# Residuals read in place, the context's low half split in two operations, and a second norm worked out from the first one's variance

## The reference, cut to what matters

```
x = x + xattn(ctx, layernorm(x), mask)      # 16 heads of 16, 256 context rows
x = x + attn(layernorm(x))                  # norms once more inside, 16 heads of 64
x = x + ffn(layernorm(x))                   # 256 -> 1024 -> 256, 8 experts
# layernorm(x) = (x - mean) / sqrt(var + 1e-5)
# inside attn: xn = (x - mu) * rsqrt(var(x) + 1e-5) * g + b;  q = xn @ Wq;  k, v = x @ Wkv
```

## Time and profile before

| | us |
|---|---|
| median of 3 runs | 1583.59 |
| lowest and highest run | 1582.69, 1585.09 |
| the profiled execution's own time | 1582.87 |
| its span in the trace | 1581.1 |

### The profile page before, as it was taken

The page is one execution under the profiler, slowest core; times in us unless marked ns, Lnnn a source line. Parts: engine busy times, 40 slices in busy tenths (PEclk is TensorE's granted clock), DMA queues, the critical chain, the costliest instruction groups (busy, mean ns, idle before and its releaser), DMA issues.

```text
span 1581.1 us, 42702 instructions
## 1 busy us (share of the span) xinstructions
PE 1406.5 (89%) x16891; PEld 1024.8 (65%) x16891; DVE 1243.2 (79%) x3414; ACT 1123.3 (71%) x3091; POOL 491.3 (31%) x589
## 2 busy tenths in 40 slices
PE   3378999999999999999999999999999999999975
PEld 1245776766677666666776766667666666776744
DVE  2647888888888888888888888888888888888862
ACT  2656778777777787777778777777787777778741
POOL 2122233333323332333233333323332333233220
PEclk7589999999999999999999999999999999999987
DMA  8522212222221122222212222221122222212100
GB/s 199 171 68 75 64 42 63 70 78 79 79 79 47 43 69 78 79 78 79 70 39 60 69 78 79 78 79 53 42 65 78 78 78 79 75 37 57 52 4 7
DMA packets 80918, 110.49 MB, mean 70 GB/s; under 512 B 7592, under 2 KB 62928, under 8 KB 80720
## 3 DMA queue, kind: packets, MB, share of 16 engines
q1 hardware_dynamic: 80720, 107.76, 23.8%
HBM read 69.66 MB, written 29.69 MB: 63 GB/s over the span
## 4 chain that ended last, share of the span: by engine, by line
PE 58%; ACT 29%; DVE 8%; issue 3%; DMA 1%; POOL 1%; SPq 0%; POOLq 0%; ACTq 0%; DVEq 0%
ACT S L924 7%; PE ps_a L507 7%; PE ps_a L508 6%; PE ps_a L509 6%; ACT av L986 5%; ACT pT L936 4%; PE ps_f L507 4%; PE ps_f L509 4%; PE ps_f L508 4%; PE ps_t L597 3%; PE ps_a L728 3%; PE ps_o L609 3%; ACT aqT L1040 3%; ACT a_work L997 2%; PE ps_s L507 2%
## 5 line engine op out<-in xcount | busy, mean ns | idle before, releaser
L924 ACT ACTIVATE S<-S,x_nmx 128x256 f32<-128x256 f32 x512 | 257.0, 506 | 29.9 <-DVE x_nmx L1204 28.3
L1204 DVE CUSTOM_DVE_ANT_0 S<-ps_s,bias 128x256 f32<-128x256 f32 x512 | 201.8, 418 | 65.2 <-PE ps_s L587 63.7
L597 PE MATMUL ps_t<-ident,S 128*128 128x128 f32 x1024 | 188.9, 287 | 42.8 <-ACT S L924 26.3
L1568 POOL TENSOR_TENSOR a_len<-a_len,half 128x16 f32<-128x16 f32 x64 | 212.4, 3318 | 5.3
L936 ACT ACTIVATE pT<-ps_t 128x256 f32<-128x256 f32 x512 | 174.2, 380 | 40.6 <-PE ps_t L597 35.8
L597 PEld LDWEIGHTS ps_t<-ident,S 128*128 128x128 f32 x1024 | 115.3, 143 | 86.3 <-ACT S L924 69.5
L1573 POOL TENSOR_TENSOR aN<-aS,a_sum 128x128 f32<-128x128 f32 x32 | 30.0, 936 | 368.7 <-DVE a_sum L1305 368.7
L587 PE MATMUL ps_s<-kst,qst 128*128 128x256 f16 x512 | 115.5, 279 | 17.8 <-DMA qst<-q_hbm 15.4
L507 PE MATMUL ps_f<-zT,f_loraB 128*128 128x128 f16 x512 | 102.8, 220 | 8.7 <-ACT f_h L1028 8.6
L508 PE MATMUL ps_f<-zT,f_loraB 128*128 128x128 f16 x512 | 102.4, 219 | 0.0
L509 PE MATMUL ps_f<-zT,f_loraB 128*128 128x128 f16 x512 | 102.4, 219 | 0.0
(11 more groups left out here) (244 smaller groups left out, 4643.6 us busy)
## 6 DMA issues: line engine op xcount, KB each, us to landing
ctxT<-in_ctxT SPq DMA_DIRECT2D x32, 512.0 KB, 4.8
k_hbm<-kT SPq DMA_DIRECT2D x32, 512.0 KB, 3.0
kst<-k_hbm SPq DMA_DIRECT2D x32, 512.0 KB, 4.4
kst<-negm SPq DMA_DIRECT2D x32, 256.0 KB, 3.1
q_hbm<-qT SPq DMA_DIRECT2D x64, 128.0 KB, 1.8
kst<-k_hbm SPq DMA_DIRECT2D x32, 256.0 KB, 3.4
qst<-q_hbm SPq DMA_DIRECT2D x32, 256.0 KB, 4.6
x_ld<-in_x SPq DMA_DIRECT2D x32, 128.0 KB, 4.2
```

Of the source, the lines that this page charges most:

```text
L597: last = turn(ps_t[t % 2][:, c * P:(c + 1) * P], S[:, t % S_BUFS, c * P:(c + 1) * P], ident[:])
L924: go(S[:, t % S_BUFS, :], S[:, t % S_BUFS, :], ACT.Exp, bias=x_nmx[:, t:t + 1], scale=-1.0, accum_out=x_sum[:, t:t + 1]).then_inc(sem["exp ...
L1204: nc.vector.tensor_tensor_reduce(out=S[:, t % S_BUFS, :], in0=ps_s[t % 2][:, 0:TK], in1=bias[:, pair, :], scale=-1.0, scalar=BIG, op0=ALU. ...
L1568: tt(ln, ln, half[:, 0:AH], ALU.pow).then_inc(sem["a_len"], 1)
```

## The change

There are three edits and a new order.

- **No residual copies.** `x_ld`, `x1` and `x2` become pairs of buffers, used by turns, and the residual is added from them. The three POOL copies go. The load of `x` for unit `u` waits for `x1` of unit `u - 2` where it waited for the norm and the copy of unit `u - 1`.
- **The context's low half in two operations.** POOL's one operation on 1024 numbers becomes two on 512. `x_k` waits for both.
- **The second norm from the first variance.** The normed row has mean zero and variance `v * r * r`, where `v` and `r` are the first norm's variance and factor. POOL works out the second factor from them in three small operations, and DVE's second pass of statistics goes.

```diff
-                    pe.wait_ge(sem["ctx_split"], at("ctx_split", u, 2))
+                    pe.wait_ge(sem["ctx_split"], at("ctx_split", u, 3))
...
-                dve.wait_ge(sem["x_kept"], at("x_kept", u, 1))
-                if seen(u - 1):
-                    dve.wait_ge(sem["a_kept"], at("a_kept", u - 1, 1))
-                stt(x1[:], ps_o[:, 0:D], DOWN, x_res[:], ALU.mult, ALU.add).then_inc(sem["x1_ready"], 1)
+                stt(x1[u % 2][:], ps_o[:, 0:D], DOWN, x_ld[u % 2][:], ALU.mult, ALU.add).then_inc(sem["x1_ready"], 1)
...
+                    dve.wait_ge(sem["a_normed"], at("a_normed", u, 1))
+                    dve.wait_ge(sem["a_rstd"], at("a_rstd", u, 5))
+                    ts(a_n[:], a_x[:], a_rs[:, 1, 1:2], None, ALU.mult).then_inc(sem["a_normed"], 1)
...
-            def x_split_ctx(u):
-                pool.wait_ge(sem["ctx_split"], lone(pool, "ctx_split", u, 1))
-                tt(ctxS[:, 1].rearrange("p c n -> p (c n)"), ctxT[:].rearrange("p c b k -> p (c b k)"),
-                   ctxS[:, 0].rearrange("p c n -> p (c n)"), ALU.subtract).then_inc(sem["ctx_split"], 1)
-
-            def x_keep(u):
-                pool.wait_ge(sem["x_loaded"], lone(pool, "x_loaded", u, 16))
-                if seen(u - 1):
-                    pool.wait_ge(sem["x1_ready"], lone(pool, "x1_ready", u - 1, 1))
-                pool.tensor_copy(x_res[:], x_ld[:]).then_inc(sem["x_kept"], 1)
+            def x_split_ctx(u, n):
+                pool.wait_ge(sem["ctx_split"], at("ctx_split", u, 1))
+                tt(ctxS[:, 1, n], ctxT[:, n].rearrange("p b k -> p (b k)"), ctxS[:, 0, n], ALU.subtract)\
+                    .then_inc(sem["ctx_split"], 1)
...
+                    pool.wait_ge(sem["a_rstd"], at("a_rstd", u, 2))
+                    ts(a_mv[:, 1, 0:1], a_mv[:, 0, 1:2], a_rs[:, 0, 1:2], None, ALU.mult).then_inc(sem["a_rstd"], 1)
+                    pool.wait_ge(sem["a_rstd"], at("a_rstd", u, 3))
+                    ts(a_rs[:, 1, 0:1], a_mv[:, 1, 0:1], a_rs[:, 0, 1:2], EPS, ALU.mult, ALU.add).then_inc(sem["a_rstd"], 1)
+                    pool.wait_ge(sem["a_rstd"], at("a_rstd", u, 4))
+                    tt(a_rs[:, 1, 1:2], a_rs[:, 1, 0:1], half[:, 0:1], ALU.pow).then_inc(sem["a_rstd"], 1)
```

All three tables of slots have new numbers too, so nearly every engine's order changes. Two rows of `SLOT` as an example:

```diff
-    pe_x_k=(-30, -28), pe_x_out=(-28,), pe_x_v=(-26, -24), pe_x_turn=(-28,), pe_x_q=(-27,), pe_x_turn_inv=(70,),
+    pe_x_k=(-30, -30), pe_x_out=(-30,), pe_x_v=(-27, -18), pe_x_turn=(-30,), pe_x_q=(-29,), pe_x_turn_inv=(83,),
```

More of the change, by code:

```diff
@@ L93 @@
+    pool_x_mask=(63,), pool_x_split_ctx=(87, 94),
 )
 FIRST = dict(
[L95 to L99 removed]
@@ L229, in build @@
         null_len, half = sb("null_len", [AH * NNULL, 2]), sb("half", [P, 2 * AH])
-        x_ld, x_res, x_n = sb("x_ld", [P, D]), sb("x_res", [P, D]), sb("x_n", [P, D])
+        x_ld, x_n = [sb(f"x_ld{n}", [P, D]) for n in range(2)], sb("x_n", [P, D])
         ctxT, mask32, negm = sb("ctxT", [P, KD, BU, TK]), sb("mask32", [32, BU * TK // 4], I32), sb("negm", [32, BU * TK], F16)
@@ L245, in build @@
         oT = split("oT", [P, KD, BU, TQ])
-        x1 = sb("x1", [P, D])
-        a_res, a_x, a_n = sb("a_res", [P, D]), sb("a_x", [P, D]), sb("a_n", [P, D])
+        x1 = [sb(f"x1_{n}", [P, D]) for n in range(2)]
+        a_x, a_n = sb("a_x", [P, D]), sb("a_n", [P, D])
         a_st, a_mv, a_rs = sb("a_st", [P, 2, 6]), sb("a_mv", [P, 2, 2]), sb("a_rs", [P, 2, 2])
@@ L264, in build @@
         aP, aN = sb("aP", [P, AH, TQ]), sb("aN", [P, 4, AH, NNULL])
-        x2 = sb("x2", [P, D])
-        f_res, f_n, f_out = (sb(n, [P, D]) for n in ("f_res", "f_n", "f_out"))
+        x2 = [sb(f"x2_{n}", [P, D]) for n in range(2)]
+        f_n, f_out = (sb(n, [P, D]) for n in ("f_n", "f_out"))
         f_st, f_mv, f_rs = sb("f_st", [P, 6]), sb("f_mv", [P, 2]), sb("f_rs", [P, 2])
@@ L1167, in x_stats @@
                 dve.wait_ge(sem["x_loaded"], at("x_loaded", u, 16))
-                stats(u, x_ld[:], x_st[:], x_mv[:], "x_stats", 0)
+                stats(u, x_ld[u % 2][:], x_st[:], x_mv[:], "x_stats", 0)
             def x_norm(u):
                 dve.wait_ge(sem["x_rstd"], at("x_rstd", u, 2))
-                norm(x_ld[:], x_n[:], x_mv, x_rs).then_inc(sem["x_normed"], 1)
+                norm(x_ld[u % 2][:], x_n[:], x_mv, x_rs).then_inc(sem["x_normed"], 1)
             def rest(to, of, less):
@@ L1402, in f_final @@
                 dve.wait_ge(sem["y_sum"], at("y_sum", u, 1))
-                dve.wait_ge(sem["f_kept"], at("f_kept", u, 1))
-                stt(f_out[:], f_out[:], g_1[:, 3:4], f_res[:], ALU.mult, ALU.add)\
+                stt(f_out[:], f_out[:], g_1[:, 3:4], x2[u % 2][:], ALU.mult, ALU.add)\
                     .then_inc(sem["out_ready"], 1)
@@ L1585, in _ @@
             x_rstd(0)
-            x_split_ctx(0)
-            x_keep(0)
+            x_split_ctx(0, 0)
+            x_split_ctx(0, 1)
             x_mask(0)
@@ L1601, in step @@
                             a_length(ua, n)
-                    if do_x:
-                        for n in due(table, "pool_x_keep", s):
-                            if not (isinstance(i, int) and i == 0):
-                                x_keep(i)
-                    if do_a:
-                        for n in due(table, "pool_a_keep", s):
-                            a_keep(ua)
                         for n in due(table, "pool_a_scale_nulls", s):
                             a_scale_nulls(ua)
-                    if do_f:
-                        for n in due(table, "pool_f_keep", s):
-                            f_keep(uf)
                     if ahead:
```

142 lines of the change are left out of this document (65 added, 77 removed).

## The result

The changed kernel takes **1593.59 us** (median of 7 executions, 1587.51 to 1594.91), the kernel before 1583.27 (7 executions, 1580.7 to 1585.09): a ratio of 1.0066, 95% interval 1.0055 to 1.0077. It is slower by 0.66%, 10.3 us. The profiled execution took 1594.75 with a span of 1592.9, against 1582.87 and 1581.1 before. So 11.8 us of span have to be found.

What follows compares the result with a forecast made beforehand. PE was saturated early in each step, ACT's order set the second part, with the seam also open. Thirty steps +2.4, head +1.5, tail -1.3, together +2.6 on 1582.87: 1585.5 us; own range 1580 to 1590, overall 1571 to 1597.

Steps and rivals of the forecast that it cites:

- The edits at nothing: Steps 1 to 31: dropped POOL copies, dropped second statistics and the relaxed load wait were costed at nothing.
- Steps 2 and 3: Mid-step: first `x_turn_probs` gains 0.66 us; ACT idles 0.85, keys wait about 1.0, `a_spread` ends about 0.3 later.
- Step 4: Self-attention softmax to step end: 0.34 us lateness, half won back on DVE; PE's list gives 45.38, 0.17 shorter.
- The lateness of `a_scores` is not won back: Rival: the 0.34 us carries through to the last exponential, 30 x 0.3 = +9, so 1592; chance 0.15.
- Step 5: Seam between steps: POOL's two halves end later and start the next step, `x_k` at 774.87, a step of 45.63.
- the step's term: Steps in the loop: +0.08 us each on 45.55, 30 x 0.08 = +2.4 in the sum.
- Head: Step 0: `x_invT` copy behind two ACT splits starts DVE's splits 3.4 us later, half taken up: +1.5, between 0 and +3.4.
- Tail: Step 32 and after: `a_k` ahead of `a_turn` -0.8, `hT` no longer ahead of `a_copy_probs` -0.5: -1.3, between 0 and -2.
- the rival in which `x_norm` is shut out: Seam: POOL's second half takes the ports before `x_norm`; step 46.43, 30 x 0.88 = +26, so 1609; chance 0.09.

Runs made afterwards that it cites:

- edits_old_order: The three edits with the kernel before's order in all three tables: 1581.63 us, ratio 0.9997 to the kernel before.
- copy_v_first: Changed kernel with ACT's first copy of `a_v` ahead of the first exponential again: 1587.87 us, ratio 1.0029 to the kernel before.
- mix_stats_gap: Changed kernel with step 0's old order, ACT's first `a_v` copy before the first exponential, first scores behind `zr`'s transposes, statistics of `x` directly before `x_inv`: 1575.74 us.
- last_old: Changed kernel with the order of before in steps 32 and 33 alone: 1593.8 us, ratio 1.0075 to the kernel before.
- stats_early: Changed kernel with DVE's statistics of `x` ahead of the last two biases again: 1605.1 us, ratio 1.0139 to the kernel before.
- key_turn_late: Changed kernel with PE's second turn of the keys behind the third `x_turn_probs`: 1592.35 us, ratio 1.0059 to the kernel before.
- scores_fill: Changed kernel with PE's second `a_scores` behind the next three groups of `x_turn_probs` and `x_scores`: 1655.99 us, ratio 1.0464 to the kernel before.

## Why the prediction was right, and where not

1585.5 was forecast, with 1571 to 1597 as the range and slower at 0.36. The time lies in that range, but outside the forecast's own 1580 to 1590 and 8.1 us above the forecast. The direction was no more likely than the other in the prediction (faster had 0.37), and the loss is four times the +2.6 of the sum. In the two traces the sum's three terms, +2.4, +1.5 and -1.3, came out as +4.2, +4.1 and +3.5: the range held because it was wide, not because the sum was right. By its steps:

**The edits at nothing**: right, edits_old_order shows it (0.9997).

**Steps 2 and 3, the trade on ACT**: the mechanism is right. ACT was to idle 0.85 us and idles 0.70; the end of `aqT` (`a_spread`) was to move by 0.3 and moved by 0.35; the keys were to wait 1.0 and wait 0.87. (The prediction took 1.57 us for a call of `a_copy_v` whose row says 1.55; nothing hangs on it.)

**Step 4, "half is won back"**: the step that failed, and not where it looks. `x_inv` was to start 0.30 us earlier and starts 0.21 earlier, so on that chain the later statistics do win about what was said of them (0.54 in copy_v_first, where nothing is late). Wrong is the next sentence, "PE's own list then ends so that `x_turn` can start at 774.40". From 732.70 that is 41.70 us; `x_turn` starts at 41.93, 0.23 late. PE's list, 0.34 late, reaches `x_inv` only 0.86 us behind the end of that operation (0.31 before), so it is the late `a_scores` that sets the end of the step, as in the rival "The lateness of `a_scores` is not won back" (0.15). Taking the cause away (copy_v_first) gives 0.31 back. With the lateness gone the step is 45.35, which is 0.19 under 45.54. The forecast's 45.38 was meant to hold in the changed kernel; it holds only without the edit to ACT's order that it was to include. So the rival's size was wrong as well: it counted +0.3 on the old step and should have counted it on 45.35.

**Step 5, the seam**: wrong. 0.25 us was forecast between PE's list and POOL's halves; the changed kernel has 0.01, mix_stats_gap saved 0.02. The halves came as forecast (2.33 us for two), `x_norm` got between them as forecast, but PE arrives as late as they do, since the lateness of step 4 holds it. `x_k` was to start 42.17 us behind `x1` and starts at 42.20. That the step's term, +0.08, lies so near the measured +0.13 is luck: `x_turn` comes 0.23 later than forecast, and `x_k` follows it by 0.27 where 0.47 was forecast.

**Head, +1.5 between 0 and 3.4**: mis-sized, +4.1 at step 2, outside its own bounds. The mechanism (the copy of `x_invT` behind two splits) is there. The row of splits was to start 3.4 late and started 4.63 late. Half of it was to be taken up, "because the load for the last piece is what is waited for". But that load is issued only when DVE's split of `a_wo` has ended, at 73.56 for 67.61, and so the wait moved with it. Missing from the sum was also that both meetings with POOL's halves, 0.97 us each, now stand ahead of that load.

**Tail, -1.3 between 0 and -2**: in the trace -0.1 to the last `x2` (-0.9 against last_old, which differs only in that table) and then +3.6 by the clock, which no term of the sum had.

**The ports.** The rule of the Trainium skill ("SBUF — State Buffer", section "Who interferes with whom"), that whichever instruction is first has the shared ports to its end, held: `x_n` (0.72 us, and 0.41 in stats_early, where POOL is done before it) fitted between two halves, the second `f_out` took 0.81 us for 0.49, and two splits of weights took 3.25 for 2.28. In the changed kernel no step showed the rival in which `x_norm` is shut out (46.43). Some steps of copy_v_first are as long as that, by the wait for `qst`, with `x_n` in its place. In mix_stats_gap `x_n` does end 0.15 us behind the second half, in each step, and costs nothing, since the halves are early.

## What to carry to other kernels

When a wait moves from one place to another, follow the engine that was waited for, not the one that waits: here ACT's pause of 0.70 us went down a chain of ACT, DVE and PE and cost 0.31 in the usual step, while the waits on PE could be pushed about (key_turn_late) at no gain, or at a great loss (scores_fill). When a load is sometimes late, look at what stands behind the instruction that waits for it: work that another engine needs belongs ahead of it. Two transposes moved there took away every long step, with the load as late as before (1365.7 to 1360.2 us for thirty steps, 1580.47 to 1575.09 in all). Before a wait for a load is counted as a cushion, see what issues the load. And take the fixed parts at both ends as seriously as the loop: 7.6 of the 11.8 us lay there in these traces.

## What the runs showed of the hardware

The same matmuls in the same order can meet a different TensorE clock at the end of a kernel. By windows of 1 us it rose in the kernel before at about 1564.3, 3 us after the first expert matmul (1561.3), and in the changed kernel at about 1582.2, 12.4 us after it (1569.8). From `x2` to the end the traces take 30.1 us (three, all with the old `LAST`) or 31.9 to 33.7 (all others). What in the work before decides it is not settled by these runs, nor is how often either happens: last_old has the short end in its trace and the changed kernel's median.

DVE's splits of 2048 numbers took 2.28 us alone and 3.25 beside POOL's two halves (4.73 us together, 2.33 in a usual step); beside the old operation of 4.08 us an operation on 272 columns took 2.36, and 0.53 in the changed kernel, behind both halves. Splitting POOL's work did not take the collision away (1.9 us longer in all, 1.8 before) but put it on two operations.
